# Two mixture-of-experts stages and one causal attention stage: half of the expert rows added by ScalarE and GpSimd, fronts and one low part reordered

## What is computed

```python
x = x + _L0_attn_a_ref(_layernorm(x), ...)   # segmented linear attention with a memory
x = x + _L0_ffn_ref(_layernorm(x), ...)
x = x + _L0_attn_b_ref(_layernorm(x), ...)   # causal attention, 16 heads of 128
x = x + _L0_ffn_ref(_layernorm(x), ...)
x = x + _L1_attn_a_ref(_layernorm(x), ...)   # causal grouped-query attention, heads of 16
x = x + _L1_ffn_ref(_layernorm(x), ...)
x = x + _L1_attn_b_ref(_layernorm(x), ...)
x = x + _L1_ffn_ref(_layernorm(x), ...)
```

## Time and profile before

| what | us |
|---|---|
| median of three runs | 1680.42 |
| lowest and highest run | 1674.7, 1683.16 |
| the profiled execution's own time | 1682.4 |
| its span in the profile | 1680.5 |
| TensorE busy in it | 1465.1 (87%) |
| VectorE busy | 913.4 (54%) |
| ScalarE busy | 754.4 (45%) |
| GpSimd busy | 412.1 (25%) |

### The profile page before, as it was taken

How to read it: one execution, slowest core, us unless ns; L and a number is a source line. 1 busy time by engine, 2 the same in 40 slices (tenths; PEclk the granted TensorE clock), 3 DMA queues, 4 the chain that set the end, 5 groups by cost and what they waited for, 6 DMA issues and landing times. The chain is left out here.

```text
span 1680.5 us, 27965 instructions
## 1 busy us (share of the span) xinstructions
PE 1465.1 (87%) x10122; PEld 1107.5 (66%) x10128; DVE 913.4 (54%) x1972; ACT 754.4 (45%) x1872; POOL 412.1 (25%) x328
## 2 busy tenths in 40 slices
PE   5999999997799789999899878978887797899598
PEld 4778887776677657767677657765554576533476
DVE  5766666664631846555565555157554514376722
ACT  5574656553344243443434433433443343577243
POOL 2607043120235321110211011721000461100173
PEclk9999999998899899999999989979998899899799
DMA  4002020100613410010010041330000523000433
GB/s 149 31 3 86 2 64 27 51 2 1 234 50 102 143 39 32 1 44 0 13 31 1 1 174 63 100 104 13 1 1 15 204 92 109 1 1 1 175 97 122
DMA packets 43141, 99.96 MB, mean 59 GB/s; under 512 B 7184, under 2 KB 21904, under 8 KB 42896
## 3 DMA queue, kind: packets, MB, share of 16 engines
q1 hardware_dynamic: 33040, 70.05, 12.3%
q0 software_dynamic: 9984, 28.32, 5.2%
HBM read 80.00 MB, written 18.35 MB: 59 GB/s over the span
## 5 line engine op out<-in xcount | busy, mean ns | idle before, releaser
L856 DVE TENSOR_TENSOR s_h_e<-s_bank,s_silu_e 128x176 f32<-128x176 f32 x92 | 31.2, 341 | 184.3 <-ACT s_silu_e L638 184.3
L506 PE MATMUL s_bank<-s_expert_w,s_xe 128*128 x368 | 128.3, 472 | 1.4 <-ACT s_xe L632 0.7
L132 POOL TENSOR_SCALAR ln_var<-ln_moments 128x4 f32<-128x4 f32 x16 | 4.0, 253 | 482.3 <-DVE ln_moments L117 283.4
L371 POOL DMA_INDIRECT s_xg<-normed_rows,s_from_row x92 | 92.4, 1005 | 113.7 <-DVE s_from_row L762 86.9
L378 POOL DMA_INDIRECT expert_rows<-s_y,s_to_row x92 | 91.1, 990 | 100.0 <-ACT s_y L650 83.0
L2584 POOL TENSOR_TENSOR s_w_hi<-s_w_raw,zero 128x1024 fp32r<-128x1024 f32 x25 | 55.6, 2223 | 212.3 <-PE s_memory L80 188.0
L1209 ACT ACTIVATE s_scratch<-s_bank,s_neg_max 128x128 f32<-128x128 f32 (+3 forms) x128 | 67.2, 528 | 89.1 <-DVE s_neg_max L1299 89.1
L530 PE MATMUL s_bank<-s_expert_w,s_he 88*128 x368 | 96.1, 383 | 4.9 <-ACT s_he L644 4.9
L1299 DVE TENSOR_REDUCE s_neg_max<-s_bank 128x1 f32<-128x128 f32 (+3 forms) x128 | 59.7, 488 | 74.2 <-PE s_bank L1112 74.0
L1129 PE MATMUL s_bank<-s_probs_t,s_v 128*128 128x512 f32 (+3 forms) x256 | 76.7, 442 | 20.2 <-ACT s_probs_t L1217 20.2
L1110 PE MATMUL s_bank<-s_k,s_q 128*128 128x128 f32 (+3 forms) x256 | 90.0, 447 | 3.0 <-ACT s_scratch L1209 2.2
(11 more groups left out here) (390 smaller groups left out, 4270.9 us busy)
## 6 DMA issues: line engine op xcount, KB each, us to landing
s_expert_w<-in_experts SPq DMA_DIRECT2D x32, 608.0 KB, 12.7
s_w_raw<-in_wa_o SPq DMA_DIRECT2D x16, 512.0 KB, 3.6
s_yg<-expert_rows SPq DMA_DIRECT2D x32, 256.0 KB, 4.5
s_raw<-in_shared SPq DMA_DIRECT2D x16, 384.0 KB, 7.1
normed_rows<-s_ln_xn POOLq DMA_DIRECT2D x8, 512.0 KB, 9.3
s_w_raw<-in_wa_k SPq DMA_DIRECT2D x4, 512.0 KB, 4.1
s_w_raw<-in_wa_v SPq DMA_DIRECT2D x4, 512.0 KB, 3.5
s_w_raw<-in_wa_q SPq DMA_DIRECT2D x4, 512.0 KB, 4.5
```

What stands on the lines that cost most here:

```text
L371: pool.indirect_dma_start(out=xg[:, i % XG_RING, :], out_offset=None, in_=x_rows[:, :], in_offset=bass.IndirectOffsetOnAxis(ap=from_row[:, ...
L506: last = pe.matmul(u_bank[i % 2][:, 0:2 * INTER], xe[:, i % 2, x], expert_of(P, i, w), start=c == 0, stop=c == DC - 1, skip_group_check=True)
```

## The change

It has three parts.

1. **Tails of the early stages.** For token tiles 4 to 7 (pairs 2 and 3) ScalarE multiplies the rows of both choices by their weights (eight activations of 128x256, behind the stage's last high part), GpSimd adds the two choices (128x512) and then adds the sum to x (128x512), twice, behind its last scatter. VectorE's `add_tiles(2)` and `add_tiles(3)` go, and its `add_shared(2)` and `add_shared(3)` wait for GpSimd (`far_added`). VectorE does `h_of(5)` and `h_low(5)` ahead of `add_tiles(1)`.
2. **Fronts of the early stages.** VectorE does `h_of(0, 1)` ahead of the ranks, and both `h_low(0, ...)` ahead of reading the lists. TensorE no longer waits for `rows_known` ahead of `down(0)`: it clears banks 1 to 3, does token tiles 2 to 7, and only then waits, clears bank 0 and does tiles 0 and 1. In all four feed-forward stages `down` waits for the low part of the half of the tokens that it is about to read, not for both halves.
3. **Causal stage.** `low_o(U - 1)` stands ahead of the first maximum of row tile 1, not behind it.

```diff
@@ -309,6 +309,7 @@
         diagonal_done, second_added = sem("diagonal_done"), sem("second_added")
         by_vector = TOP_K if early else 1
         stored = sem("out_stored")
+        weights_done, rows_scaled, rows_summed, far_added = sem("weights_done"), sem("rows_scaled"), sem("rows_summed"), sem("far_added")
         xg_loaded = [sem(f"xg_loaded{r}") for r in range(XG_RING)]
         xt_ready, xe_done, e_loaded = sem("xt_ready"), sem("xe_done"), sem("expert_w_loaded")
         u_ready, silu_e_done, h_e_done = sem("u_ready"), sem("silu_e_done"), sem("h_e_done")
@@ -387,6 +388,15 @@
                 scatter(i)
                 if i + XG_RING < TILES:
                     gather(i + XG_RING)
+            if early:
+                for n in range(NT // 4, NT // 2):
+                    two = slice(2 * n, 2 * n + 2)
+                    pool.wait_ge(rows_scaled, 2 * TOP_K * (n - NT // 4 + 1))
+                    pool.tensor_tensor(yg[:, 0, two, :], yg[:, 0, two, :], yg[:, 1, two, :], ALU.add).then_inc(rows_summed, 1)
+                    pool.wait_ge(rows_summed, n - NT // 4 + 1)
+                    pool.wait_ge(acc_read, n + 1)
+                    pool.tensor_tensor(res.x[:, two, :], yg[:, 0, two, :], res.x[:, two, :], ALU.add).then_inc(far_added, 1)
+
         @block.tensor
         def _(pe):
             def fill(bank, column, n, half):
@@ -411,9 +421,12 @@
                     pe.wait_ge(h_done, 2 * n + half - 1)
                 fill(up_bank[half], SH_UP, n, half).then_inc(up_ready, 1)
 
-            def down(n, last_of_run):
-                pe.wait_ge(h_lo_done, 2 * n + 2)
-                for t in range(NT):
+            def down(n, last_of_run, order=range(NT)):
+                for t in order:
+                    pe.wait_ge(h_lo_done, 2 * n + t // TB + 1)
+                    if n == 0 and early and t == 0:
+                        pe.wait_ge(rows_known, 1)
+                        clear_acc(acc[0:1])
                     at = slice(t * P, (t + 1) * P)
                     k = rows_of(n)
                     last = product(pe, acc[t // 2][:, t % 2 * D:(t % 2 + 1) * D],
@@ -424,8 +437,8 @@
                         last.then_inc(acc_ready, 1)
                 last.then_inc(w_used, 1)
 
-            def clear_acc():
-                for bank in acc:
+            def clear_acc(some=acc):
+                for bank in some:
                     pe.matmul(bank[:], res.zeros[:, 0:P], res.zeros[:], start=True, stop=False, skip_group_check=True)
 
             def rank():
@@ -473,10 +486,9 @@
                 up(1, 0)
                 up(1, 1)
             list_rows()
-            pe.wait_ge(rows_known, 1)
             if early:
-                clear_acc()
-                down(0, False)
+                clear_acc(acc[1:])
+                down(0, False, (2, 3, 4, 5, 6, 7, 0, 1))
                 for n in range(2, n_first):
                     up(n, 0)
                     up(n, 1)
@@ -664,6 +677,13 @@
                 if i + 1 < TILES:
                     h_out(i + 1)
             shared_run(range(n_first, n_shared))
+            if early:
+                act.wait_ge(weights_done, 1)
+                for n in range(NT // 4, NT // 2):
+                    act.wait_ge(y_back[n], 16 * TOP_K)
+                    for k in range(TOP_K):
+                        for t in (2 * n, 2 * n + 1):
+                            act.activation(yg[:, k, t, :], yg[:, k, t, :], ACT.Copy, scale=token_w[:, t, k:k + 1]).then_inc(rows_scaled, 1)
 
         @block.vector
         def _(dve):
@@ -724,6 +744,7 @@
                     low(n)
             if early:
                 h_of(0, 0)
+                h_of(0, 1)
 
             dve.wait_ge(ranked, 1)
             then(dve.tensor_scalar(full[:], rank_bank[:, NT * N_EXP:(NT + 1) * N_EXP], float(P - 1), None,
@@ -750,8 +771,8 @@
                 dve.tensor_tensor(slot_hit[:, some, :], slot_iota[:].unsqueeze(1).broadcast_to([P, ROWS // 2, P]),
                                   spread(in_slot[:, some], P), ALU.is_equal).then_inc(slot_hit_done, 1)
             if early:
-                h_of(0, 1)
                 h_low(0, 0)
+                h_low(0, 1)
             dve.wait_ge(listed, 1)
             found = list_bank[:, 0:3 * TILES].rearrange("p (a i) -> p a i", a=3)
             dve.scalar_tensor_tensor(spare[:], found[:, 2, :], 1.0, spare_row, ALU.subtract, ALU.mult).then_inc(spare_done, 1)
@@ -760,9 +781,7 @@
             dve.wait_ge(spare_done, 1)
             then(dve.tensor_tensor(to_row[:], row[:], spare[:], ALU.subtract))
             dve.tensor_scalar(from_row[:], to_row[:], TOK - 1, None, ALU.bitwise_and).then_inc(rows_known, 1)
-            if early:
-                h_low(0, 1)
-            else:
+            if not early:
                 h_of(0, 0)
                 h_of(0, 1)
             then(dve.tensor_reduce(upto[:], before[:, 1, :, :], AX.X, ALU.add))
@@ -794,7 +813,10 @@
                 else:
                     dve.wait_ge(w_used, ends)
                 if ends == n_shared:
-                    dve.wait_ge(y_added, 2 * by_vector * (b + 1))
+                    if early and b >= NT // 4:
+                        dve.wait_ge(far_added, b - NT // 4 + 1)
+                    else:
+                        dve.wait_ge(y_added, 2 * by_vector * (b + 1))
                 if owner_is_gated:
                     for t in (2 * b, 2 * b + 1):
                         last = dve.scalar_tensor_tensor(res.x[:, t, :], acc[b][:, t % 2 * D:(t % 2 + 1) * D], gate_exp[:, t:t + 1],
@@ -842,6 +864,7 @@
                 then(dve.tensor_tensor(token_w[:], chosen[:], spread(row_sum[:], TOP_K), ALU.mult))
             else:
                 then(dve.tensor_copy(token_w[:], chosen[:]))
+            dve.sem_inc(weights_done, 1)
             if not early:
                 dve.tensor_tensor(weight_diagonal[:], res.ident[:].unsqueeze(1).broadcast_to([P, NT, P]), spread(token_w[:, :, 1], P),
                                   ALU.mult).then_inc(diagonal_done, 1)
@@ -867,14 +890,14 @@
                 h_low(n_first, half)
             add_tiles(0)
             if early:
-                h_of(n_shared - 1, 0)
-            add_tiles(1)
-            if early:
-                h_of(n_shared - 1, 1)
+                for half in range(NHALF):
+                    h_of(n_shared - 1, half)
                 for half in range(NHALF):
                     h_low(n_shared - 1, half)
-            add_tiles(2)
-            add_tiles(3)
+            add_tiles(1)
+            if not early:
+                add_tiles(2)
+                add_tiles(3)
             add_shared(0, 2 if early else 1)
             add_shared(1, 2 if early else 1)
             measure(0)
@@ -1928,11 +1951,10 @@
                     row_max(U + 1, 2, 1)
                 if U + 2 < UNITS:
                     split_q(U + 2)
-                if ahead:
-                    row_max(U + 1, 1, 0)
                 if U:
                     low_o(U - 1)
                 if ahead:
+                    row_max(U + 1, 1, 0)
                     row_max(U + 1, 1, 1)
                     row_max(U + 1, 0, 0)
                     row_max(U + 1, 0, 1)
```

## The result

The changed kernel takes 1661.52 us (median of four runs, 1658.02 to 1665.47), against 1679.63 for the kernel before on the same occasion (four runs, 1674.7 to 1683.16). The ratio is 0.9895, with an interval of 0.9861 to 0.9929: 18 us faster. The prediction was 25.5 us. Its sign is right, and the time lies in the range, but the terms did not come out alike. The profiled execution took 1661.48 us, with a span of 1659.7.

A forecast was written before the change was run, and what follows sets the result against it. TensorE, busy in 87% of the span, bounds the kernel, with time won at its waits, low clock and stage ends; 7.2 + 4.0 + 4.9 + 9.4 = 25.5 us off the median of 1680.42 gives 1655, range 1644 to 1670.

The forecast's parts named there:

- Fronts: Early stages' starts: TensorE's waits go and piece 2 begins 3.6 us earlier per front, 7.2 us (4.2 to 9.6).
- the same work as before (4.91 us): Front: TensorE's work from the clears to piece 2 keeps its 4.91 us, ending at 452.2 rather than 455.84.
- Tails: Early stages' ends: VectorE loses eight additions, 3.26 us, less a 1.28 us block; 2.0 per tail, 4.0 (1.4 to 6.6).
- VectorE sets the end: Tail: VectorE ends last, so removing TensorE's 1.9 us wait per stage was costed at nothing.
- the third rival: Tail: GpSimd's four additions, p each, become the bound; the kernel is slower from p = 4.8 us, up to 1693.5; chance 0.02.
- Causal stage: Earlier `low_o` saves 0.82 us of wait in six units, 4.9 us; fewer clock falls give 9.4 us.
- the rival of 14.3: Causal stage, stated before `low_o_only`: a fall costs 2.3 us and four go, 14.3 us faster; no chance given.
- costing the moved maximum at nothing: Causal stage: the maximum behind `low_o` starts at 1178.75 instead of 1178.31, not late, as TensorE waits for no maximum.
- The clock term: Causal stage: four of five clock falls go, at 2.3 us a fall, for 9.4 us (0 to 11.7).
- 14.31 without one: Causal stage: low parts 14.31 us apart without a clock fall, against 16.65 with one, so 2.3 us a fall.
- near 13.5 to 14 us: Causal stage, sign of success: the distance from one low part to the next comes near 13.5 to 14 us.
- The first rival: Causal stage: the clock falls all the same, so the gain is 16.1 us, giving 1664.3; chance 0.20.

The follow-up runs named there:

- fronts_only: The kernel before with only the changed fronts and the finer waits of `down`; ratio 0.9941 (0.9915 to 0.9966).
- low_o_only: The kernel before with only `low_o` moved ahead of one maximum; ratio 0.9906 (0.9875 to 0.9937).
- tails_only: The kernel before with only the changed tails of the early stages; ratio 1.0005 (0.9984 to 1.0027).
- pool_waits_last: The kernel before with GpSimd waiting, without further work, for the last shared sum's reading at the end of both early stages; ratio 1.004 (1.0016 to 1.0064).
- half_tail: The changed kernel with ScalarE and GpSimd doing pair 2 only and VectorE pair 3 again; ratio 0.9878 (0.9855 to 0.99).
- f_no_h_of: The changed kernel with `h_of(0, 1)` behind `slot_hit` again; ratio 0.9917 (0.9889 to 0.9945).
- after_again: The changed kernel measured once more, beside the version with three GpSimd additions, against the kernel before; ratio 0.9888 (0.9846 to 0.993), median 1664.01 us.

## Why the prediction was right or wrong

**Fronts, forecast 7.2 us: mechanism right, size too small.** The waits went where the prediction said. The step that was mis-sized is "the same work as before (4.91 us)": it kept a clock of 0.50 that the changed front never shows. At 1.00 the same work takes 3.7 us (3.48 in the first profile, where one clear has no record). That is 1.2 of the 1.6 us by which a front beat its forecast; the rest is that the clears began 8.5 us after the first `h_full` rather than 8.8. The upper bound of 4.8 per front was passed too (5.2). Taken from the eight old fronts in four profiles, of which six were long and two short, a new one saves 4.5 us on the average, 9 in two; `fronts_only` measured 9.9 (6 to 14).

**Tails, forecast 4.0 us: wrong, it is a loss of 1.2.** The additions (1.28 forecast), the block of VectorE (1.28 forecast, 1.05 measured) and the order were right within 0.3 us. ScalarE's eight activations took 3.30 us, not 2.7, and GpSimd was done 12.9 us after the last `h_full`, not 12.5. The step that failed is "VectorE sets the end" together with the formula of the third rival, "the stage ends at 549.85 + 4p + 0.84". It took a stage to be over when the last sum is. What really ends it is the later of two: VectorE's last sum plus 1.36 us, and GpSimd's last step plus 5.3 us. With p = 1.3 GpSimd was no bound inside the stage, and yet it decided the tail. So the third rival named the right engine, but for the wrong price. The earlier trace rows and the row at 560.29 held the hint, a barrier that closed in 1.36 us with GpSimd idle for 21.62; nothing in the trace of before gave the other case.

**Finer waits, forecast nothing.** The finer waits of `down` in the two late feed-forward stages are in no run by themselves. Leaving out the occasion with 1712.94, those stages took 107.4 to 110.5 us in the profiles with the old waits and 107.2 to 110.0 with the finer ones, so no effect shows.

**Causal stage, forecast 4.9 + 9.4 = 14.3 us.** `low_o_only` measured 15.8 (10.5 to 21), so the sum is confirmed, its parts less so; of what I expected before that run, 7 to 12 us was low, and the rival of 14.3 was nearer. The wait gave 5.5 (8.2 to 2.7), a little more than 4.9. The prediction's ground for costing the moved maximum at nothing was misread: TensorE did wait for maxima before, eight times and 3.2 us in all, of which the earlier trace rows show no row. The changed kernel has the same eight waits with the same 3.2 us, so the move cost nothing all the same. The clock term was taken as four falls of 2.3 us. The step "14.31 without one" compared unequal units: between 1252.41 and 1266.72 TensorE was busy for 11.58 us, in a full clean unit of the changed kernel (1204.58 to 1218.92) for 12.96. For the same reason the sign "near 13.5 to 14 us" failed, with 14.36 measured. These are the low parts of `low_o_only`, with a fall in the first unit and none in the third, which have the same work (152 products each; the second has 176), and the windows of its clock:

```profile
1177.00 0.69 DVE L1872 TENSOR_TENSOR s_o_lo<-s_pair,s_o_hi 128x512 fp32r<-128x512 f32 x1
1192.91 0.69 DVE L1872 TENSOR_TENSOR s_o_lo<-s_pair,s_o_hi 128x512 fp32r<-128x512 f32 x1
1210.40 0.69 DVE L1872 TENSOR_TENSOR s_o_lo<-s_pair,s_o_hi 128x512 fp32r<-128x512 f32 x1
1224.75 0.69 DVE L1872 TENSOR_TENSOR s_o_lo<-s_pair,s_o_hi 128x512 fp32r<-128x512 f32 x1
```

```profile
1179.70:1183.10 3.40, 3.40 (x28) 1.05 (x24) 0.82 (x4) 0.48 (x2) 0.00 (x0) 0.51 0.00 0
...
1213.90:1217.30 3.40, 3.30 (x42) 1.72 (x37) 0.45 (x3) 1.10 (x3) 0.00 (x0) 1.00 0.02 5
```

15.91 less 14.35 is 1.6 us a fall. More of them went, however, and some were double: the profiles of `tails_only` and `fronts_only` show the clock down in all six units, in two of them for twice as long, and `pool_waits_last` in five, as the kernel before; the ten profiles with `low_o` ahead show it down in none to two. The first rival, that the clock falls all the same, is thus refuted. The profiled execution of the kernel before had one of the milder patterns, so the pair of first profiles shows only 7.6 us for this stage. Over all profiles the stage took 171.0 to 178.3 us with the old order (four, mean 174.8) and 160.8 to 164.6 with the new (ten, mean 162.4), 12.4 us apart.

**Sum.** The parts measured alone are 9.9 + 15.8 - 0.8 = 24.9 us, while the changed kernel gained 18 (12 to 23) and, without its tails, 22 (16 to 27). These agree within their intervals. Of the 7 us that the forecast missed, the tails account for 5.2, which is shown. The fronts came out larger than forecast, so they hid a part of that, and the total lies in the range although one of its terms had the wrong sign. By the profiles alone the parts are 9.0 (fronts) + 12.4 (causal stage) - 1.2 (tails) = 20.2 us, 2 more than measured. I can't place these 2, since the stages that the change doesn't touch vary as much between two profiles (the attention between the early stages by 2.0).

## What to carry to other kernels

Before you give work to an idle engine near the end of a stage, look at what the barrier behind it costs with that engine busy to the end; in this kernel GpSimd finished 1.1 us ahead of VectorE, and the next stage then began 2.9 us later behind VectorE, more than the 2.3 us that the moved work had gained. Take a reference for "the clock at full" from a unit that has the same work, and look at several executions, since one profile shows only one pattern of falls. A short wait removed ahead of a long run of TensorE's can be worth more than its length where the clock had fallen behind it: with the 2.8 us wait put back, the front took 3.0 us more, an estimated half of them by the clock.

## What the runs showed of the hardware that I had not expected

- GpSimd needs about 5.3 us from its last step in one block to the first in the next: 5.26 to 5.29 us in all fourteen tails with additions in which it set the end, and a gap of 5.49 and 5.39 behind a mere wait. Where GpSimd was done early enough, 6.3 us ahead of VectorE in `half_tail` and longer elsewhere, VectorE's last sum is followed by the next stage in 1.26 to 1.38 us. No DMA packet is recorded in the gap. Which of the steps between takes it (the clearing of semaphores, the barrier, the way from one block to the next) the profile doesn't record, and that wasn't tried.
- The same wait of 2.8 us in front of the same work was followed by 6.8 us at a clock of 0.50 in six old fronts and by none in two, 2.6 us apart. In the two of `f_no_h_of` it was 3.4 us.
- The addition of two 128x512 tiles took GpSimd 1.26 to 1.30 us undisturbed, and up to 1.43 beside or right behind VectorE's additions from SBUF. VectorE paid 1.04 to 1.05 us for each meeting. Once, in `after_again`, it was GpSimd that paid: its first addition took 1.62 us, and VectorE's four 1.67.
